# Rope products at other key tiles, and the shared-key maxima ending one tile sooner, in a four-layer transformer kernel

## The chip, the cores and the metric

The kernel runs on one core of one Trainium2 chip. The metric is device time in microseconds (us). A core has TensorE for matmuls (PE in the profile), VectorE (DVE), ScalarE (ACT), GpSimd (POOL) and SyncE (SP), which issues most DMAs. Each engine works through its own instructions in order; semaphores hold one engine back for another.

## The reference

Four layers, each `x + attention(layernorm(x)) + feed-forward(layernorm(x))`, on 1024 tokens of 256 features. The change touches only the two attentions of layer 0, both causal, with 16 heads of 16 features:

```python
# latent attention with rotary positions ("rope")
ql = x @ Wqd
q  = (ql @ Wqu)                      # 16 heads x 16
qr = apply_rope(ql @ Wqr, cos, sin)  # 16 heads x 64: x*cos + rotate_half(x)*sin
kr = apply_rope(x @ Wkr, cos, sin)   # one key of 64 for all heads
scores = (q @ k.T + qr @ kr.T) * scale
out = softmax(causal(scores)) @ v @ Wo
# feed-forward of layer 0: attention whose key and value are shared by all heads
k_shared, v_shared = the routed head's k and v, v weighted by the gate
att = softmax(causal(q @ k_shared.T / 4))
y = att @ v_shared                   # for each of 16 heads
```

## The kernel before, in words

The 16 heads of each attention go in groups of four. `GROUPS[0]` is the eight groups i = 0 to 7 of layer 0: even i are the latent attention (`is_mla`, here "rope groups"), odd i the shared-key attention (`is_shared`), in turn. Each group loops over eight key tiles kt of 128 keys. (i,kt) names a tile of this loop. For a tile PE computes transposed scores into psA (lines 1687 and 1688; a unit is one head for kt below 4 and two heads above), ACT turns them into exponentials in Pr (lines 912, 917), POOL masks the diagonal block (line 781), and PE multiplies with the values into psO (`values_product`, line 1725) one tile later. Since only queries from kt x 128 on are scored, later tiles are shorter.

The softmax needs each row's maximum beforehand. So, while group i runs, PE computes the plain scores of a group ahead once more into the two psD banks (`maxima_unit`, lines 1670 and 1672), in 38 units, and DVE reduces each unit (line 1204). `max_window` says beside which tiles the units of a group run, `beside` shares them out in proportion to the tiles' widths. A rope group's maxima run in tiles 0 to 4 of the shared-key group before it; a shared-key group's begin in tiles 5 to 7 two groups before it and end in the rope group before it. `max_end` is the tile at which they are complete. At that tile DVE negates the maxima (line 1209), PE transposes them (line 1678), DVE copies the row out (line 1222), and ACT sends it by DMA (`maxima_row`, lines 931 and 934) into the query operand, as one more row of it. For a shared-key group it is `Qs<-mrowb`. PE waits for it (`mrow_in`) before the group's first score.

Queries of the rope attention are rotated in products of two heads each, `rope` 0 to 7. 0 to 3 (heads 0 to 7) are made at the start. 4 to 7 (heads 8 to 15, for groups 4 and 6) are made beside the tiles of `ROPE_AT`: eight PE matmuls in four units (`rope_unit`, line 1604), four DVE products with cos and sin (line 1183), then on POOL, after that tile's mask, a sum (line 736), on ACT, after the next tile's exponentials, a rounded copy (line 944), and on POOL, after the next tile's mask, the remainder (line 741). SP stores both parts to HBM (`store_rotated`: `d_qr<-WB`, `d_qr<-xnT`), the remainder's product waiting in the places WB or xnT.

SP's program for a rope group i in 2 and 4: wait for and store products i+2 and i+3, wait until the stores have landed, wait until the scores of tile 3 of group i are filled, then load the first half of group i+2's high parts (`load_high`: `Qr<-d_qr`, `Qr<-d_qn`, `Kr<-d_kn`); once all scores of group i are filled, the second half and the rest. PE waits for the first half before the first maxima unit of group i+2, in tile 0 of group i+1. SP takes all this in order.

In group 6 POOL also carries the butterflies of a weight transform (line 792), two after each mask.

Of the kernel before, what the change touches and what calls it, by code (L numbers as in the profile page):

```python
# [53 lines left out]

def max_end(g):

    return 5


def is_mla(i):  # L60
# [4 lines left out]
def is_shared(i):  # L65

    return i < 2 * NG and i % 2 == 1
# [4 lines left out]
    return i // 2 if i < 2 * NG else i - 2 * NG  # L72


ROPE_AT = {(2, 0): 4, (2, 2): 5, (4, 0): 6, (4, 2): 7}
KV_AT = {(0, 0): range(0, NT // 2), (0, 1): range(NT // 2, NT)}
KEY_KT = 3

# [1 line left out]
def beside_products(i, kt):  # L80

    if (i, kt) in KV_AT:
        return [("kv", j) for j in KV_AT[i, kt]]
    if (i, kt) in ROPE_AT:
        return [("rope", ROPE_AT[i, kt], k) for k in range(4)]
    if (i, kt) == (2 * NG - 1, 1):
# [4 lines left out]
def max_window(i, first):  # L91

    if i == 1:
        return [(0, kt) for kt in range(KEY_KT, max_end(1))]
    tail = [(i - 2, kt) for kt in range(max_end(i - 1), NT) if i - 2 >= first and not is_mla(i)]
    return tail + [(i - 1, kt) for kt in range(max_end(i))]
# [24 lines left out]
def build(nc, ins, out):  # L121
    with ExitStack() as ctx:
# [575 lines left out]
        def _(pool):  # L698
# [34 lines left out]
            def rope_add(p):  # L733
                pool.wait_ge(d_drained, DU[f"rope{p}"])
                v, b = rope_place(p)
                pool.tensor_tensor(v, v, b, ALU.add).then_inc(rope_sum, 1)

            def rope_rest(p):
                pool.wait_ge(rope_high, p + 1)
                v, b = rope_place(p)  # L740
                pool.tensor_tensor(v.bitcast(F32R), v, b, ALU.subtract).then_inc(rope_low, 1)
# [34 lines left out]
            def mask_exponentials(i, kt):  # L776

                s = NT * i + kt
                pool.wait_ge(a_drained, scored(i, kt))
                block_ = Pr[:, (s % 2) * GH * T:(s % 2 + 1) * GH * T].rearrange("p (h t) -> p h t", h=GH)[:, :, tile_cols(kt)]  # L780
                pool.affine_select(out=block_, in_=block_, pattern=[[0, GH], [1, P]], compare_op=ALU.is_ge, fill=0.0,  # L781
                                   base=0, channel_multiplier=-1).then_inc(masked, 1)
# [15 lines left out]
            for i in GROUPS[0]:  # L798
                for kt in range(NT):
                    mask_exponentials(i, kt)  # L800
                    if (i, kt) in ROPE_AT:
                        rope_add(ROPE_AT[i, kt])
                    if (i, kt - 1) in ROPE_AT:
                        rope_rest(ROPE_AT[i, kt - 1])
                    if i == 1 and kt < 4:
# [1324 lines left out]
```

## Time and profile before

| | us |
|---|---|
| median of 3 runs | 992.88 |
| lowest, highest | 991.86, 996.1 |
| the profiled execution's own time | 994.7 |
| its span | 993.0 |
| PE busy | 862.0 (87%) |
| DVE busy | 555.9 (56%) |
| ACT busy | 386.8 (39%) |
| POOL busy | 224.9 (23%) |

The groups of layer 0 run from 93.7 us on; group 7 ends near 471 us. The mean granted TensorE clock is 0.914 of full speed.

How to read the views. The chain is the path of work that ended last, followed back from the end. A timeline row is the start, the length, engine and line, operation, out<-in with shapes, the count, and in brackets the engine's idle time before it with what ended it. A windows row is a stretch and its length, then the busy time (and instructions) of PE, PE's weight loads, DVE, ACT and POOL, then the granted clock of TensorE, the DMA engines' mean share and GB/s. A row by line and shape has the count, busy time, mean ns of one, and idle time before. A row of DMA queues has packets, MB and the share of the 16 engines. "q" behind an engine's name is its sequencer, which issues DMAs. Matmul lengths overlap, as they are pipelined; spacing of starts is the better measure.

### The profile page before, as it was taken

What the parts mean: (1) busy time and instruction counts of PE and PEld (TensorE: products, weight loads), DVE (VectorE), ACT (ScalarE), POOL (GpSimd) and SP (SyncE); (2) the same over time, 40 slices, a digit from 0 to 9 for tenths busy, and PEclk for the clock granted to TensorE, in tenths of its full rate; (3) what the DMA queues carried; (4) which work ended last, traced back from release to release, by engine and by line L of the source; (5) the groups of instructions that cost most, each with busy time, mean ns of one, the idle gap of its engine ahead of it and who ended that gap; (6) DMA issues with size and microseconds to landing.
All of it is one profiled execution on the core that took longest, in us unless ns stands there. A gap on an engine that the chain in (4) does not pass through costs nothing.

```text
span 993.0 us, 11940 instructions
## 1 busy us (share of the span) xinstructions
PE 862.0 (87%) x4799; PEld 505.4 (51%) x4799; DVE 555.9 (56%) x991; ACT 386.8 (39%) x476; POOL 224.9 (23%) x207
## 2 busy tenths in 40 slices
PE   4697979988999899987779998788999889888997
PEld 2354434444344434524448886533333258687776
DVE  4574486774677476512433453596777337934452
ACT  2504314534444454445351331205555754500340
POOL 2661002323013212523010100500111147600000
PEclk9878999999799889979789997968999989989899
DMA  6687216514721770020400002759000061000001
GB/s 174 130 174 225 34 33 107 112 49 105 129 34 43 145 179 2 2 71 1 149 0 1 1 1 88 147 108 130 2 2 1 2 222 43 0 1 1 1 1 43
DMA packets 35648, 66.82 MB, mean 67 GB/s; under 512 B 5908, under 2 KB 14652, under 8 KB 35524
## 3 DMA queue, kind: packets, MB, share of 16 engines
q1 hardware_dynamic: 35016, 65.92, 29.0%
q8 instruction: 38, 0.62, 0.3%
q10 hardware_dynamic: 576, 0.13, 0.1%
q14 instruction: 18, 0.15, 0.1%
HBM read 45.93 MB, written 16.29 MB: 63 GB/s over the span
## 4 chain that ended last, share of the span: by engine, by line
PE 63%; DVE 19%; DMA 6%; ACT 6%; POOL 2%; issue 2%; SPq 1%; ACTq 0%; DVEq 0%; POOLq 0%
PE psA L1604 11%; PE psD L1604 11%; PE psO L1725 10%; DVE mx L1204 9%; PE psD L1670 8%; PE psA L1688 7%; PE psO L1604 7%; PE psA L1687 3%; DMA Kr<-d_kn 3%; DVE hid_low L1518 2%; PE psD L1672 2%; PE psA L1636 1%; SPq L488 1%; ACT Pr L912 1%; PE psD L1736 1%
## 5 line engine op out<-in xcount | busy, mean ns | idle before, releaser
L1204 DVE TENSOR_REDUCE mx<-psD 128x1 f32<-128x512 f32 (+3 forms) x416 | 259.3, 659 | 122.9 <-PE psD L1672 88.3
L912 ACT ACTIVATE Pr<-psA 128x1024 f32<-128x1024 f32 (+3 forms) x192 | 161.9, 865 | 194.9 <-PE psA L1688 185.4
L781 POOL TENSOR_SCALAR_AFFINE_SELECT Pr<-Pr 128x512 f32<-128x512 f32 x96 | 61.0, 635 | 435.6 <-ACT Pr L912 349.6
L917 ACT ACTIVATE Pr<-psA 128x1024 f32<-128x1024 f32 (+3 forms) x96 | 63.5, 702 | 65.4 <-PE psA L1688 65.0
L1725 PE MATMUL psO<-Pr,Vh 128*32 128x512 f32 (+3 forms) x768 | 81.9, 507 | 3.7 <-POOL Pr L781 3.0
L1687 PE MATMUL psA<-Qr,Kr 128*128 128x512 f32 (+3 forms) x192 | 77.5, 417 | 3.7 <-DMA Qr<-mrow 3.7
L1672 PE MATMUL psD<-maskq,identb 128*128 128x128 bf16 x348 | 73.0, 234 | 0.0
L1688 PE MATMUL psA<-Qr,Kr 113*128 113x512 f32 (+3 forms) x192 | 66.5, 354 | 0.0
L1670 PE MATMUL psD<-Kg,Qs 96*128 96x512 bf16 (+3 forms) x192 | 56.2, 333 | 9.0 <-DVE mx L1204 6.9
L1670 PE MATMUL psD<-Kr,Qr 80*128 80x512 bf16 (+3 forms) x166 | 59.2, 390 | 5.2 <-DVE mx L1204 3.0
L1688 PE MATMUL psA<-Qs,Kg 97*128 97x512 bf16 (+3 forms) x192 | 51.3, 366 | 9.5 <-DMA Qs<-mrowb 4.3
L1670 PE MATMUL psD<-Ks,Qs 96*128 96x512 bf16 (+3 forms) x166 | 53.5, 351 | 4.6 <-DVE mx L1204 3.8
L1688 PE MATMUL psA<-Qs,Ks 97*128 97x512 bf16 (+3 forms) x192 | 45.8, 332 | 5.3 <-ACT Pr L912 3.3
L1670 PEld LDWEIGHTS psD<-Kg,Qs 96*128 96x128 bf16 x192 | 17.9, 97 | 57.8 <-DVE mx L1204 43.8
L1687 PEld LDWEIGHTS psA<-Qr,Kr 128*128 128x128 f32 x192 | 37.6, 196 | 18.2 <-ACT Pr L917 6.2
L1636 PE MATMUL psA<-identf,xn 128*128 128x128 f32 x96 | 21.6, 389 | 27.2 <-DVE xn L1169 26.7
L1670 PEld LDWEIGHTS psD<-Kr,Qr 80*128 80x128 bf16 x166 | 18.0, 109 | 50.2 <-DVE mx L1204 37.1
L1725 PE MATMUL psO<-Pr,Vg 128*32 128x512 f32 (+3 forms) x384 | 42.7, 525 | 0.6 <-POOL Pr L781 0.5
L1670 PEld LDWEIGHTS psD<-Ks,Qs 96*128 96x128 bf16 x166 | 16.4, 100 | 47.3 <-DVE mx L1204 42.2
L1672 PEld LDWEIGHTS psD<-maskq,identb 128*128 128x128 bf16 x348 | 36.8, 106 | 5.9 <-issue 3.3
L1688 PEld LDWEIGHTS psA<-Qr,Kr 113*128 113x128 f32 x192 | 37.3, 194 | 4.2 <-issue 1.9
L1604 PE MATMUL psA<-xnT,WA 128*128 128x512 f32 x56 | 32.2, 739 | 2.7 <-ACT xnT L877 2.2
(403 smaller groups left out, 1658.6 us busy)
## 6 DMA issues: line engine op xcount, KB each, us to landing
Qr<-d_qr SPq DMA_DIRECT2D x18, 512.0 KB, 12.3
d_qr<-WB SPq DMA_DIRECT2D x9, 512.0 KB, 2.6
Pr<-d_cb SPq DMA_DIRECT2D x8, 512.0 KB, 7.8
Qs<-d_gq SPq DMA_DIRECT2D x24, 128.0 KB, 4.8
Qs<-d_q SPq DMA_DIRECT2D x24, 128.0 KB
Ks<-d_k SPq DMA_DIRECT2D x24, 128.0 KB
Qr<-d_qn SPq DMA_DIRECT2D x18, 128.0 KB, 7.7
Kr<-d_kn SPq DMA_DIRECT2D x18, 128.0 KB, 8.5
```

Of the source, the lines that this page charges most:

```text
L781: pool.affine_select(out=block_, in_=block_, pattern=[[0, GH], [1, P]], compare_op=ALU.is_ge, fill=0.0, base=0, channel_multiplier=-1).the ...
L912: act.activation(place[:, h, q0:T], src[:, q0:T], ACT.Exp, scale=score_scale(i)).then_inc(a_drained, 1)
L917: act.activation(place[:, h:h + 2, q0:T], src[:, :, q0 - HALF:HALF], ACT.Exp, scale=score_scale(i)).then_inc(a_drained, 1)
L1204: dve.tensor_reduce(mx[:, j, part, h0:h0 + nh], src, AX, ALU.max).then_inc(d_drained, 1)
L1518: dve.tensor_tensor(hid2_low[:, m - DC, :], slot(Qs, m - DC), hid2_high[:, m - DC, :], ALU.subtract).then_inc(hid2_split, 1)
L1604: op = pe.matmul(dst, lhsT, rhs, start=start and k == 0, stop=stop and k == len(terms) - 1)
L1636: op = pe.transpose(dst[:, tile_cols(j)], src[:, j, c * P:(c + 1) * P], identf[:])
L1670: op = pe.matmul(dst[:, k * w:(k + 1) * w], q, kk, start=True, stop=not diagonal)
L1672: op = pe.matmul(dst[:, (k + 1) * w - P:(k + 1) * w], identb[:], maskq[:], start=False, stop=True)
L1687: pe.matmul(out_, second[0], second[1](lo, (half + 1) * HALF), start=True, stop=False)
L1688: op = pe.matmul(out_, k, q(lo, (half + 1) * HALF), start=second is None, stop=not (diagonal and mask))
L1725: op = pe.matmul(psO[h * VW:(h + 1) * VW, lo:hi], values(i, kt, h), e, start=kt == 0, stop=kt == last_kt, tile_position=(0, h * VW), skip_ ...
```

## The change

`max_end` is 4 instead of 5 for the shared-key groups 3, 5 and 7; for group 1 and all others it stays. So groups 2, 4 and 6 have no maxima units beside tile 4, the 38 units are shared out over one tile less, and the row is transposed and sent in tile 4. `ROPE_AT` puts rope products 4 and 6 beside tile 5 of groups 1 and 3, and 5 and 7 beside tile 0 of groups 2 and 4. Nothing is added or left out.

```diff
 def max_end(g):
 
-    return 5
+    return 4 if is_shared(g) and g > 1 else 5
...
-ROPE_AT = {(2, 0): 4, (2, 2): 5, (4, 0): 6, (4, 2): 7}
+ROPE_AT = {(1, 5): 4, (2, 0): 5, (3, 5): 6, (4, 0): 7}
```

Units of maxima beside each tile of group 2 (the same in 4 and 6), and of tile 7 of the group before:

| | (1,7) | (2,0) | (2,1) | (2,2) | (2,3) | (2,4) |
|---|---|---|---|---|---|---|
| before | 1 | 8 | 8 | 6 | 5 | 5 |
| now | 2 | 9 | 8 | 8 | 6 | 0 |

PE in group 2 where the maxima of group 3 are transposed (`identf,mneg`), before. The 128x384 rows are scores of tile 5, the 128x256 row of tile 6:

```order
L1687 MATMUL psA<-Qr_51,Kr_52 128x384
L1688 MATMUL psA<-Qr,Kr 128x384
L1678 MATMUL psD<-identf,mneg 32x128
L1725 MATMUL psO<-Pr,Vh 32x512 x4
L1687 MATMUL psA<-Qr_51,Kr_52 128x256
L1688 MATMUL psA<-Qr,Kr 128x256
```

And now. The 128x512 rows are scores of tile 4:

```order
L1687 MATMUL psA<-Qr_51,Kr_52 128x512
L1688 MATMUL psA<-Qr,Kr 128x512
L1678 MATMUL psD<-identf,mneg 32x128
L1725 MATMUL psO<-Pr,Vh 32x128 x4
L1725 MATMUL psO<-Pr,Vh 32x512 x4
L1687 MATMUL psA<-Qr_51,Kr_52 128x384
L1688 MATMUL psA<-Qr,Kr 128x384
```

The transposition stands ahead of tile 5's scores, not behind them.

DVE from the last maxima of group 2, in (1,4), to the outputs of group 1 in (2,1), before. L1183 are the rope products, `mneg` and `mrow` group 2's row:

```order
L1209 TENSOR_REDUCE mneg<-mx 128x32
L1222 CAST mrow<-psD 32x128
L1204 TENSOR_REDUCE mx<-psD 128x4
L1204 TENSOR_REDUCE mx<-psD 128x2 x2
L1204 TENSOR_REDUCE mx<-psD 128x1 x3
L1183 TENSOR_TENSOR WB<-psD,gate 128x512 x4
L1204 TENSOR_REDUCE mx<-psD 128x1 x9
```

And now:

```order
L1209 TENSOR_REDUCE mneg<-mx 128x32
L1222 CAST mrow<-psD 32x128
L1183 TENSOR_TENSOR WB<-psD,gate 128x512 x4
L1204 TENSOR_REDUCE mx<-psD 128x4
L1204 TENSOR_REDUCE mx<-psD 128x2 x2
L1204 TENSOR_REDUCE mx<-psD 128x1 x4
L1183 TENSOR_TENSOR WB<-psD,gate 128x512 x2
L1183 TENSOR_TENSOR xnT<-psD,gate 128x512 x2
L1204 TENSOR_REDUCE mx<-psD 128x1 x8
```

Product 4 stands right behind group 2's row, in (1,5), and product 5 (the one with `xnT`) in (2,0), where 4 stood.

ACT from group 2's row to its tile 3, before. L944 is a rope product's rounded copy; L917 with 2x256 and 2x128 are the exponentials of (1,6) and (1,7), L912 with 1024, 896, 768, 640 those of (2,0) to (2,3):

```order
L931 DMA Qr<-mrow 1x32x128
L917 ACTIVATE Pr<-psA 128x2x256 x2
L917 ACTIVATE Pr<-psA 128x2x128 x2
L912 ACTIVATE Pr<-psA 128x1024 x4
L962 ACTIVATE OT<-psO 128x1024
L912 ACTIVATE Pr<-psA 128x896 x4
L944 ACTIVATE WB<-WB 128x1024
L912 ACTIVATE Pr<-psA 128x768 x4
L912 ACTIVATE Pr<-psA 128x640 x4
L944 ACTIVATE xnT<-WB 128x1024
```

And now:

```order
L931 DMA Qr<-mrow 1x32x128
L917 ACTIVATE Pr<-psA 128x2x256 x2
L944 ACTIVATE WB<-WB 128x1024
L917 ACTIVATE Pr<-psA 128x2x128 x2
L912 ACTIVATE Pr<-psA 128x1024 x4
L962 ACTIVATE OT<-psO 128x1024
L912 ACTIVATE Pr<-psA 128x896 x4
L944 ACTIVATE xnT<-WB 128x1024
L912 ACTIVATE Pr<-psA 128x768 x4
L912 ACTIVATE Pr<-psA 128x640 x4
```

The first copy now stands between the exponentials of (1,6) and (1,7), the second behind (2,1). On POOL the sum stands ahead of the mask of (1,6) and the remainder ahead of that of (1,7). SP's instructions and their order are the same.

## Rows read from the trace of the kernel before

**Rows 1.** chain that ended last, shares of the span by engine
```profile
PE 63%; DVE 19%; DMA 6%; ACT 6%; POOL 2%; issue 2%; SPq 1%; ACTq 0%; DVEq 0%; POOLq 0%
```

**Rows 2.** windows: group 0 to 1, group 2 to 3 (two rows), group 4 to 5
```profile
156.92:173.51 16.59, 15.22 (x110) 6.42 (x109) 12.69 (x22) 9.12 (x11) 3.85 (x5) 1.00 0.94 157
241.97:267.55 25.58, 21.86 (x110) 8.94 (x109) 13.02 (x22) 9.38 (x12) 1.91 (x3) 0.67 1.00 169
245.87:267.55 21.68, 20.34 (x96) 8.46 (x97) 13.02 (x22) 8.62 (x10) 1.27 (x2) 0.61 0.98 170
334.47:359.79 25.32, 21.79 (x110) 8.88 (x109) 13.01 (x22) 9.38 (x12) 1.90 (x3) 0.66 1.08 174
```

**Rows 3.** timeline of PE, end of group 2
```profile
231.74 0.59 PE L1687 MATMUL psA<-Qr,Kr 128*128 128x512 f32 x1
...
235.94 0.39 PE L1670 MATMUL psD<-Kg,Qs 96*128 96x512 bf16 x1
...
236.22 0.38 PE L1670 MATMUL psD<-Kg,Qs 96*128 96x512 bf16 x1
...
238.06 0.28 PE L1678 MATMUL psD<-identf,mneg 128*32 128x128 f32 x1
...
242.25 0.64 PE L1725 MATMUL psO<-Pr,Vh 128*32 128x256 f32 x8
245.17 0.61 PE L1688 MATMUL psA<-Qs,Kg 97*128 97x512 bf16 x2 [2.28 <-DMA Qs<-mrowb]
246.50 0.29 PE L1670 MATMUL psD<-Kr,Qr 80*128 80x128 bf16 x1 [0.73 <-DMA Kr<-d_kn]
```

**Rows 4.** timeline of SP's queue, group 2
```profile
213.62 2.82 SPq L488 DMA_DIRECT2D d_qr<-WB  x2
...
236.03 0.32 SPq L488 DMA_DIRECT2D d_qr<-WB  x1
238.64 0.58 SPq L488 DMA_DIRECT2D Qr<-d_qr  x1
```

**Rows 5.** chain in order of time, group 2: start, length
```profile
233.63 2.38 POOL WB L741
```

**Rows 6.** DMA queues from 242.0 to 243.3; timeline of ACT
```profile
q1 hardware_dynamic: 164, 0.28, 109.9%
...
238.79 0.51 ACTq L934 DMA_DIRECT2D Qs<-mrowb  x1
```

**Rows 7.** windows: (0,4)-(0,5), (1,5)-(1,7), (2,2), (4,0), (4,2), (4,4), (6,0), (6,2)
```profile
139.25:155.07 15.82, 13.01 (x72) 6.11 (x70) 10.72 (x19) 3.67 (x5) 1.27 (x2) 0.89 0.19 34
188.24:196.12 7.88, 6.97 (x63) 3.72 (x62) 4.78 (x10) 3.25 (x6) 1.91 (x3) 1.00 0.36 113
214.91:227.15 12.24, 10.42 (x51) 4.85 (x50) 8.74 (x14) 3.24 (x5) 1.94 (x3) 0.86 0.17 70
290.15:300.05 9.90, 9.06 (x49) 5.77 (x48) 7.91 (x13) 4.90 (x6) 0.73 (x2) 1.00 0.44 53
308.93:319.64 10.71, 8.90 (x51) 4.49 (x50) 8.71 (x14) 3.25 (x5) 1.94 (x3) 1.00 0.20 80
325.93:330.00 4.07, 4.07 (x34) 2.28 (x33) 2.94 (x5) 1.93 (x4) 2.96 (x2) 1.00 0.49 198
382.38:389.78 7.40, 6.89 (x41) 4.31 (x40) 5.44 (x9) 4.89 (x5) 0.73 (x2) 1.00 0.01 2
398.65:405.45 6.80, 6.50 (x42) 3.03 (x40) 5.13 (x10) 3.25 (x4) 0.14 (x2) 1.00 0.01 2
```

**Rows 8.** DVE by line and shape, 190 to 240 us
```profile
L1204 DVE TENSOR_REDUCE mx<-psD 128x1 f32<-128x512 f32 x24 | 15.7, 688 | 5.8 <-PE psD L1670 4.1 <-PE psD L1672 1.7
...
L1183 DVE TENSOR_TENSOR WB<-psD,gate 128x512 f32<-128x512 f32 x6 | 3.9, 686 | 1.5 <-PE psD L1604 1.5
```

**Rows 9.** timelines of POOL and PE, end of group 6
```profile
417.64 0.64 POOL L781 TENSOR_SCALAR_AFFINE_SELECT Pr<-Pr 128x512 f32<-128x512 f32 x1 [0.50 <-ACT Pr L917]
...
427.05 1.03 PE L1688 MATMUL psA<-Qs,Kg 97*128 97x512 bf16 x2 [3.79 <-POOL Pr L781]
```

## The prediction

> **What bounds the kernel now.** I read the page's chain first. PE carries 63% of it; the next shares are DVE 19% and DMA 6% [rows 1]. So PE sets the end, and time goes where PE stands still or runs at the low clock. I then laid windows over the tiles of the first attention, above all where one head group hands over to the next. (i,kt) below is key tile kt of group i; groups 0, 2, 4, 6 are rope groups, 1, 3, 5, 7 shared-key groups.
>
> The windows over the handovers are the finding. Tile 7 of group 0 and the first two tiles of group 1 take 16.59 us together, at clock 1.00. The same work takes 25.58 us from group 2 to 3 and 25.32 us from group 4 to 5, at a mean clock of 0.67. Of the 25.58, tile 7 is 3.90 (25.58 less 21.68) and the two tiles after it 21.68, at clock 0.61. PE's busy time grows as well, from 15.22 to 21.86 us [rows 2], so this is slow matmuls, not only waiting. Of its two levels, 1.2 and 2.4 GHz, the clock sits at the lower for most of that stretch.
>
> What stands ahead of it is in PE's timeline. After the last product of group 2 (242.25) PE idles 2.28 us for the row of maxima, `Qs<-mrowb`, and after two matmuls another 0.73 us for `Kr<-d_kn` [rows 3]. Both are DMAs. From group 0 to 1 PE is idle 1.37 us of 16.59 in all, and the clock stays up [rows 2].
>
> Where do the two come from? SP's queue gives the second. The high parts of group 4's queries and keys (`Qr<-d_qr`, `Qr<-d_qn`, `Kr<-d_kn`) are issued from 238.64 on, behind the store `d_qr<-WB` of rope product 5 at 236.03 [rows 4]. The chain shows what the store waited for: POOL's subtraction, 2.38 us from 233.63 [rows 5]. The load is in when PE goes on at 246.50 [rows 3]. The first wait: ACT issues `Qs<-mrowb` at 238.79, and PE goes on at 245.17, 6.4 us later. It is one row. The load went out 0.15 us before it and has the DMA engines full: 164 packets of SP's queue in the 1.3 us from 242.0 [rows 3, 4, 6]. So the late load makes both waits.
>
> **The change part by part.** P is the time at which PE starts the scores of (2,4); before it is 231.74, and PE wants group 3's row when the product at 242.25 is done, 2.28 us before 245.17: at 242.9, P+11.1 [rows 3].
>
> Rope products move. Each is 8 PE matmuls, 4 DVE products of 0.69 us, two POOL passes of 2.4 us, an ACT copy, and two stores on SP [rows 5, 8]. In (4,2) the tile takes 10.71 us; (6,2), with the same scores and maxima and no rope product, takes 6.80. In group 2 it is 12.24 us at clock 0.86 [rows 7]. So it costs 3.9 and 5.4 us there. Not all of that goes: DVE is busy 8.71 against 5.13 us, 3.6 more, of which the four products are 2.8; the other 0.8 is DVE's output of the group before, stretched beside POOL's remainder pass of the product of tile 0, and that product stays. So 3.1 and 4.6 are saved. What it costs at its new place, (1,5) and (3,5), no row shows. Below is what PE alone does more in (4,0), which has a product, than in (6,0), which has none: 9.06 - 6.89 = 2.2 us busy [rows 7]. Above are the four DVE products, 2.8 us. I take 2.5, the whole difference of these two tiles, 9.90 - 7.40. Tile (2,0) keeps one product (5 in place of 4), so it is even. Sum: (2.5 - 3.1) + (2.5 - 4.6) = **-2.7 us**, bounds -4.9 (2.2, and all of 3.9 and 5.4) to -2.1 (2.8).
>
> What is queued behind the moved work: on POOL the masks of (1,6) and (1,7) now stand behind the two passes, and on ACT the exponentials of (1,7) stand behind the copy. Tiles (1,5) to (1,7) take 7.88 us together [rows 7]. (1,5) starts at 188.24, and by my estimate its scores and transposition take 1.7 us. Then DVE has the product done at 192.7 (4 x 0.69), POOL's sum ends at 195.1, ACT's copy (some 1 us) behind the exponentials of (1,6) at 196.4, POOL's difference at 198.8 and the mask of (1,7), 0.64 us [rows 9], at 199.4. PE wants that mask after two score units (1 us each) and the four rope pairs (2.2 us) of (2,0), which starts near 197: at 201. So it is hidden with about 1.6 us to spare; without that cover each us late is a us of PE, twice.
>
> Five maxima units per rope group move. The 38 units of a group are shared out by the tiles' widths, and tile 4 drops out: one more in (1,7), one in (2,0), two in (2,2), one in (2,3), none in (2,4). A unit, one psD bank, is 0.28 us on PE (235.94 to 236.22) and 0.69 us on DVE [rows 3, 8]. Where PE is the pacing engine it costs 0.28, where DVE is, 0.69. DVE is busy 5.4 of 7.4 us in (6,0) and 5.1 of 6.8 in (6,2) [rows 7], so neither holds alone; I take 0.45. Added 5 x 0.45 = 2.25; saved in (2,4), which is all PE (4.07 busy of 4.07), 5 x 0.28 = 1.4. Net +0.85 each for groups 2 and 4. Group 6 is different: POOL's butterflies fill it from (6,4) on, PE waits 3.79 us for POOL before 427.05, and only the 0.50 us that POOL idles before 417.64 can be squeezed [rows 9]. There it is 2.25 - 0.5 = +1.75. Sum **+3.4 us**, bounds +0.9 and +7.0 (at 0.28 and 0.69 a unit).
>
> Group 3's and 5's row is sent a tile sooner. In (2,4) PE does eight score matmuls of 0.24 us, then the transposition, at P+2.1; DVE should have the last maximum (0.69 us) and the negation by P+1.3. From transposition to issue took 0.73 us (238.06 to 238.79) [rows 3, 6], so the row goes out at P+2.8. Rope product 5 now stands where 4 stood, and 4 was stored at 213.62 to 216.44 [rows 4], P-15; so SP's load goes as soon as (2,3)'s scores are filled, P+0.2, and is in by P+8.1 (238.64 to 246.50 was 7.9 us). PE needs it at about P+10.3. The row collides with that load again, so I give it the whole 6.4 us it took now: P+9.2. PE wants it at P+11.1 less the 1.4 us of moved units, P+9.7. That leaves 0.5 us. Both waits go. What is late next is the second half of the load, sent when group 2's scores end; group 0's handover runs so already, within its 16.59 us.
>
> With the wait gone I expect the clock to stay up as at the end of group 0. So each of the two handovers falls to 16.59 us: from 25.58, -9.0; from 25.32, -8.7. Sum **-17.7 us**, of which the waits of 2.28 and 0.73 us, twice, are 6.0 and the rest, 11.7, is clock. If the clock does not come back, the 6.0 is all that is left. Group 0's handover is the only such row at full clock, so this term rests on it.
>
> Total: -2.7 + 3.4 - 17.7 = **-17.0 us**. The profiled execution is 994.7 us with a span of 993.0, so its successor would be 977.7; the median shown, 992.88, is 1.8 below it, and 992.9 - 17.0 = **975.9 us**.
>
> **Rivals.**
> A. *The stall shrinks but stays, and the clock with it.* The load moves forward together with the row, and it has 2.6 us more of head start; my margin is 0.5 us. If the row comes 0.7 us after P+9.7 at both handovers, the waits drop from 2.3 to 0.7, the clock still falls: -2.7 + 3.4 - 2 x (1.6 + 0.7) = -3.9, 989.0 us. For it: the 6.4 us that one row takes beside the load. Against: most of the load is through by then. The Trainium skill ("DMA: Bandwidth & Descriptors", Queues, rings and completion order) says that an engine's semaphore increment lands only after every earlier write of that engine, across its queues. By that rule more of the load now stands ahead of the row, yet the row is bound by the load's own end, P+8.1, and not by 6.4 us: the spare would be 1.6 us in place of 0.5, and A would deserve 0.05 in place of the chance below. The trace agrees in that the row came 1.3 us before the load's end, not after; I keep the chance that the 6.4 us gives.
> B. *One handover is mended, the other not*, or a short clock fall appears in a rope group: -17.0 + 7 to 9, about 984 us.
> C. *Slower: the crowded tiles pace PE by DVE and the clock falls inside the rope groups.* Tiles 0 to 3 of groups 2, 4 and 6 hold 31 units instead of 27; each makes PE idle 0.41 us (0.69 - 0.28) where DVE paces. It decides from where PE's pauses there add up to what the handover had. Price: 6.6 us of clock (PE busy 21.86 - 15.22 at the handover) in each of three groups and 15 x 0.24 = 3.6 us over my 0.45: -17.0 + 19.8 + 3.6 = +6.4, 999.3 us. For it: (0,4) and (0,5), after 38 units in two tiles, are at 0.89, (2,2) at 0.86 [rows 7]. Against: these falls cost 1 to 2 us, not 6.6, and groups 4 and 6 keep 1.00 with PE busy 83 to 96% of a tile.
> D. *Nothing changes at the handover* because SP does not send the load sooner: it still stands behind group 1's end and the store; then +0.7 is left, 993.6 us. The store of 216.44 is some 15 us before P, which speaks against it.
>
> **Numbers.** Forecast 0.67, its own range 970 to 981 (the terms' bounds give 971.2 to 980.1, and a run varies by 1 or 2); A 0.14, B 0.10, C 0.05, D 0.04. About 0.5%, 5 us, is what a measurement of this kernel tells from no change. Forecast, B and a third of A are faster: 0.82. D and the rest of A are the same: 0.13. Slower: 0.05. To leave no more than 2 in 10 out, 968 to 988.
>
> **What would show it.** In the profile after: no wait for `Qs<-mrowb` or `Kr<-d_kn` at the end of groups 2 and 4, clock 1.00 there, the three tiles near 16.6 us; the load of group 4 issued some 7 us sooner against the last tile and well apart from the stores of `d_qr`; (2,2) near 7.8 us, (1,5) to (1,7) near 10.5, (2,4) near 2.9; the wait for POOL at the start of group 7 longer than 3.8 us. I am wrong if the clock is still half after those handovers, or if DVE is busy over 90% in tiles 0 to 3 of the rope groups.

## The result, and the profile after

The changed kernel takes 977.8 us (median of 4 runs, 975.59 to 980.72) against 993.2 us (991.86 to 996.1) for the kernel before beside it. The ratio is 0.984, 95% interval 0.981 to 0.988: 15.4 us faster, where 17.0 were forecast. A second set of runs of the changed kernel gave 977.0 (ratio 0.983, 0.980 to 0.986). In the profiled executions the span falls from 993.0 to 974.5 us; these two executions took 994.7 and 976.2 us, 1.5 us above and 1.6 us below the medians.

PE still carries the chain, and the share of DMA in it is a point smaller than in [rows 1]. Shares of the span by engine, of after:

```profile
PE 64%; DVE 21%; ACT 5%; DMA 5%; POOL 2%; issue 2%; SPq 1%; DVEq 0%; ACTq 0%; POOLq 0%
```

The two handovers come first, since the forecast stood on them. Windows over tile 7 of groups 2 and 4 and the two tiles behind it, of after (stretch and length, then busy time of PE, PE's weight loads, DVE, ACT, POOL, the granted clock, DMA share, GB/s):

```profile
241.41:258.00 16.59, 15.29 (x110) 6.41 (x109) 12.70 (x22) 9.12 (x12) 1.90 (x3) 1.00 0.93 160
326.56:343.22 16.66, 15.18 (x110) 6.41 (x109) 12.70 (x22) 9.12 (x11) 1.90 (x3) 1.00 0.96 153
```

Both were 25 us and more at clocks 0.67 and 0.66 [rows 2]. They now take what group 0's handover took, with the DMA engines nearly as full as before (0.93 and 0.96 against 1.00 and 1.08).

PE's timeline at the end of group 2, of after, shows the waits gone:

```profile
232.72 0.47 PE L1687 MATMUL psA<-Qr,Kr 128*128 128x512 f32 x1
...
234.68 0.27 PE L1678 MATMUL psD<-identf,mneg 128*32 128x128 f32 x1
...
241.69 0.64 PE L1725 MATMUL psO<-Pr,Vh 128*32 128x256 f32 x8
242.26 0.60 PE L1688 MATMUL psA<-Qs,Kg 97*128 97x512 bf16 x2
242.70 0.22 PE L1670 MATMUL psD<-Kr,Qr 80*128 80x128 bf16 x1
```

P, the start of (2,4)'s scores, is 232.72. From the last product (241.69) PE goes straight on to group 3's scores (242.26) and group 4's first maxima (242.70), with no bracket behind either, where [rows 3] has 2.28 and 0.73 us. SP's queue and ACT's, of after:

```profile
219.87 0.32 SPq L488 DMA_DIRECT2D d_qr<-WB  x1
232.70 0.58 SPq L488 DMA_DIRECT2D Qr<-d_qr  x1
```

```profile
235.40 0.51 ACTq L934 DMA_DIRECT2D Qs<-mrowb  x1
```

The last part of product 5 goes to its store 12.8 us before the load, so the load goes at P (forecast P+0.2) and the row at P+2.7 (forecast P+2.8). The load's first DMA is 2.7 us ahead of the row's; before it was 0.15 us ahead [rows 4, 6].

The tiles that the units and products moved into and out of, of after: (1,5) to (1,7), (2,2), (2,4), (4,2). A tile's window, here and in [rows 7], runs from the start of ACT's first exponential of the tile to that of the next one, so an ACT instruction that is put in at the border moves the border:

```profile
187.55:198.60 11.05, 9.73 (x73) 4.93 (x72) 7.94 (x15) 4.09 (x7) 5.40 (x4) 1.00 0.24 78
...
218.57:227.42 8.85, 7.11 (x46) 3.31 (x44) 7.05 (x12) 3.24 (x5) 1.59 (x2) 1.00 0.25 101
234.00:237.17 3.17, 3.17 (x27) 1.90 (x26) 0.28 (x1) 1.94 (x2) 0.70 (x2) 1.00 0.92 217
303.73:312.56 8.83, 7.09 (x46) 3.33 (x44) 7.05 (x12) 3.24 (x4) 1.59 (x2) 1.00 0.26 103
```

Against [rows 7], (1,5) to (1,7) grew from 7.88 to 11.05 us, (2,2) and (4,2) fell from 12.24 and 10.71 to 8.85 and 8.83, and (4,4) (like (2,4)) from 4.07 to 3.17.

Where the 18.5 us between the two spans lie, by windows from one group's start to another's:

| stretch | before | after | difference |
|---|---|---|---|
| groups 1 and 2 | 87.39 | 85.17 | -2.2 |
| groups 3 and 4 | 92.27 | 85.15 | -7.1 |
| group 5 | 44.24 | 37.72 | -6.5 |
| group 6 | 40.54 | 41.99 | +1.4 |
| group 7, tiles 0 to 6 | 40.38 | 39.09 | -1.3 |
| all else | 688.2 | 685.4 | -2.8 |

The change touches the first four rows, together -14.4 us. The last two do the same work in both kernels. Of the -4.1 there, -1.3 is the clock in group 7's second tile (0.86 of full speed and 10.12 us, where it was 0.76 and 11.41). The second set of runs has a profiled execution of its own, and in it this tile is at 0.77 and 11.33 us, and the first four rows are together -13.7. So no meaning is read into the last two rows.

### The profile page after: what moved, and what is told of

Same layout as the page of the kernel before. It is cut to its first block, busy times and chain, and to the rows that moved or that the text cites. A ratio compares the mean times of both kernels' runs of the same rounds, so it can differ in the third digit from the quotient of the medians.

```text
span 974.5 us, 11941 instructions
## 1 busy us (share of the span) xinstructions
PE 845.6 (87%) x4799; PEld 498.0 (51%) x4799; DVE 555.5 (57%) x991; ACT 386.6 (40%) x476; POOL 224.4 (23%) x207
## 4 chain that ended last, share of the span: by engine, by line
PE 64%; DVE 21%; ACT 5%; DMA 5%; POOL 2%; issue 2%; SPq 1%; DVEq 0%; ACTq 0%; POOLq 0%
PE psD L1604 11%; PE psA L1604 11%; DVE mx L1204 10%; PE psO L1725 10%; PE psD L1670 8%; PE psA L1688 7%; PE psO L1604 7%; PE psA L1687 4%; DMA Kr<-d_kn 2%; DVE hid_low L1518 2%; PE psA L1636 2%; PE psD L1672 1%; SPq L488 1%; PE psD L1736 1%; ACT Pr L912 1%
## 5 line engine op out<-in xcount | busy, mean ns | idle before, releaser
L912 ACT ACTIVATE Pr<-psA 128x1024 f32<-128x1024 f32 (+3 forms) x192 | 161.7, 865 | 176.0 <-PE psA L1688 166.3
L917 ACT ACTIVATE Pr<-psA 128x1024 f32<-128x1024 f32 (+3 forms) x96 | 63.4, 702 | 68.6 <-PE psA L1688 68.3
L1672 PE MATMUL psD<-maskq,identb 128*128 128x128 bf16 x348 | 69.4, 225 | 0.0
L1670 PE MATMUL psD<-Kr,Qr 80*128 80x512 bf16 (+3 forms) x166 | 53.1, 346 | 5.0 <-DVE mx L1204 3.6
L1688 PE MATMUL psA<-Qs,Kg 97*128 97x512 bf16 (+3 forms) x192 | 46.0, 335 | 5.2 <-POOL Pr L781 3.8
L1725 PE MATMUL psO<-Pr,Vg 128*32 128x512 f32 (+3 forms) x384 | 40.5, 502 | 0.1
```

What stands on the lines that cost most here:

```text
L912: act.activation(place[:, h, q0:T], src[:, q0:T], ACT.Exp, scale=score_scale(i)).then_inc(a_drained, 1)
L917: act.activation(place[:, h:h + 2, q0:T], src[:, :, q0 - HALF:HALF], ACT.Exp, scale=score_scale(i)).then_inc(a_drained, 1)
L1670: op = pe.matmul(dst[:, k * w:(k + 1) * w], q, kk, start=True, stop=not diagonal)
L1672: op = pe.matmul(dst[:, (k + 1) * w - P:(k + 1) * w], identb[:], maskq[:], start=False, stop=True)
L1688: op = pe.matmul(out_, k, q(lo, (half + 1) * HALF), start=second is None, stop=not (diagonal and mask))
L1725: op = pe.matmul(psO[h * VW:(h + 1) * VW, lo:hi], values(i, kt, h), e, start=kt == 0, stop=kt == last_kt, tile_position=(0, h * VW), skip_ ...
```

## Experiments

My theory was that the late load alone makes both waits: the product stored late holds the load back, and the load holds the row back. The rival was that the row needs its earlier start, which only the moved maxima give. The first two kernels do one half of the change each. Each ratio is to runs of the kernel before that were made beside that kernel: their median is 994.5 us for the first four kernels, 993.1 for the next four and 993.5 for the last, on three different chips. Medians from different chips are therefore compared through their ratios, and small differences by the tiles of the traces.

**The products moved alone.**

```diff
-ROPE_AT = {(2, 0): 4, (2, 2): 5, (4, 0): 6, (4, 2): 7}
+ROPE_AT = {(1, 5): 4, (2, 0): 5, (3, 5): 6, (4, 0): 7}
```

> Only the four rope products are moved; every shared-key group's maxima end at tile 5 as before. My theory (T1): the pause at the end of groups 2 and 4 is made by the late load, which both comes late itself and holds up the row of maxima; the pause brings the low clock. With the rope products moved the load goes at P+0.2 and is through when the row is issued at P+7, so the row takes 2 to 3.5 us instead of 6.4 and PE, which wants it at P+11.1, does not wait. Handovers 16.6 us each at clock 1.00, and the cost of the moved maxima units (in the changed kernel some 1.9 us in groups 2 and 4, 1.5 in group 6) is not paid: 972.5 us, 970 to 976, which is less than the changed kernel's 977.8. Rival (T2): the row is late because it is sent late; a row takes 6.4 us here whatever runs beside it. Then it is seen at P+13.4, PE waits 2.3 us, the clock falls as before, 988 to 992 us.

Measured: 975.17 us (972.15 to 977.08), ratio 0.980 (0.977 to 0.984). Window of this kernel over the handover from group 2 to 3:

```profile
240.48:257.29 16.81, 15.17 (x110) 6.34 (x109) 12.70 (x22) 9.12 (x11) 1.91 (x3) 1.00 0.94 156
```

The handover is mended with the maxima left where they were. ACT's queue has the row at 237.30:

```profile
237.30 0.51 ACTq L934 DMA_DIRECT2D Qs<-mrowb  x1
```

and the DMA queues of this kernel, from 238.4 to 238.7, hold its 48 packets and nothing else (packets, MB, share of the 16 engines):

```profile
q10 hardware_dynamic: 48, 0.01, 13.8%
```

P is 230.24 in this trace, so the row goes out at P+7.1, as in the kernel before, and PE takes it 4.0 us later (241.33) without a wait; before, PE stood ready 4.1 us after the issue and waited. The row's packets are through 1.4 us after its issue when no load stands beside it; before, with the load beside it, they ran in the same 1.3 us as 164 packets of the load [rows 6], 3.2 to 4.4 us after the issue, and PE went on another 1.9 us later. The rival falls: the row needs no earlier start. The medians of the two kernels, 975 and 977 to 978, are too close to tell what the other half of the change costs, since the intervals of the ratios overlap; the traces do tell it (below).

**The maxima moved alone.**

```diff
 # from the changed kernel
-ROPE_AT = {(1, 5): 4, (2, 0): 5, (3, 5): 6, (4, 0): 7}
+ROPE_AT = {(2, 0): 4, (2, 2): 5, (4, 0): 6, (4, 2): 7}
```

> Only max_end is 4 for groups 3, 5 and 7; the rope products stay beside (2,0), (2,2), (4,0), (4,2). T1: the row, issued at P+2.8 with nothing beside it, comes in time, but the load still goes at about P+6.9 and is in at P+14.8, while PE wants it at P+10.3; the pause is then some 4.5 us, all of it for Kr<-d_kn, at the low clock as before. The moved units cost 5 us and what tile 4 saves is waited away: 996 to 1002 us. T2 (the sooner row is what mends the handover): the clock stays up, 978 to 983 us.

Measured: 997.71 us (993.78 to 1001.91), ratio 1.004 (1.001 to 1.006). SP's queue and PE's timeline, end of group 2, of this kernel:

```profile
236.91 0.32 SPq L488 DMA_DIRECT2D d_qr<-WB  x1
239.53 0.58 SPq L488 DMA_DIRECT2D Qr<-d_qr  x1
```

```profile
242.37 0.60 PE L1688 MATMUL psA<-Qs,Kg 97*128 97x512 bf16 x2
247.68 0.29 PE L1670 MATMUL psD<-Kr,Qr 80*128 80x128 bf16 x1 [4.71 <-DMA Kr<-d_kn]
```

The row now comes in time (no wait at 242.37), yet the wait for the load is 4.71 us (4.10 at the second handover). The stall has only changed its name, since the load still stands behind the store. The handover takes 26.41 us at clock 0.68.

**The load sent later, everything else as in the changed kernel.** Two kernels move only the point from which SP sends the first half of the load.

```diff
-sp.wait_ge(a_filled, scored(i, NT // 2 - 1))
+sp.wait_ge(a_filled, scored(i, 5 if i > 0 else NT // 2 - 1))
```

> The changed kernel, but SP sends the first half of group 4's and 6's high parts only when the scores of tile 5 of groups 2 and 4 are filled, not those of tile 3. It makes the pause again by itself, without touching PE, DVE, ACT or POOL. T1 (a pause brings the low clock): the load is in near P+13.5, PE wants it at P+10.3, so it waits some 3 us twice, and the two tiles after it run at a mean clock near 0.6 and cost 6.6 us more each: 2 x (3 + 6.6) = +19, 995 to 999 us. Rival (T3: the clock fell for something else that the change took away, as the rope matmuls of (2,2) or the denser tile 4): only the wait returns, 982 to 985 us, clock 1.00 at the handovers.

Measured: 995.14 us (991.85 to 999.23), ratio 1.000 (0.998 to 1.003): the whole gain is gone. SP's queue and PE's timeline of this kernel:

```profile
237.70 0.58 SPq L488 DMA_DIRECT2D Qr<-d_qr  x1
```

```profile
245.65 0.29 PE L1670 MATMUL psD<-Kr,Qr 80*128 80x128 bf16 x1 [2.94 <-DMA Kr<-d_kn]
```

There is one such wait per handover, 2.94 and 2.86 us. The handover's window shows what comes with it:

```profile
241.25:266.65 25.40, 21.74 (x110) 8.88 (x109) 13.02 (x22) 9.38 (x12) 1.91 (x3) 0.66 0.99 169
```

8.8 us more than in the changed kernel, of which 2.9 are the wait; the other 5.9 come with the lower clock. So the rival to a pause as the cause (T3, 982 to 985 us with the clock at 1.00) falls. With 4 in place of 5:

> As load_at_5, but with the scores of tile 4. The load goes at about P+3.1, 0.3 us behind the row, so it collides with the row as in the kernel before. T1: the row comes 6.4 us after its issue, P+9.2, just in time, the load at P+11, so PE waits under 1 us. Whether so short a pause brings the low clock is open: if not, 978 to 981 us; if so, 990 to 993 us.

Measured: 979.62 us (974.59 to 982.82), ratio 0.984 (0.980 to 0.988). SP's queue and PE's timeline of this kernel:

```profile
235.02 0.58 SPq L488 DMA_DIRECT2D Qr<-d_qr  x1
```

```profile
242.86 0.23 PE L1670 MATMUL psD<-Kr,Qr 80*128 80x128 bf16 x1
...
335.91 0.63 PE L1670 MATMUL psD<-Kr,Qr 80*128 80x512 bf16 x2 [0.53 <-DMA Kr<-d_kn]
```

The first tile after the handover is just served, and the clock stays at 1.00 over both handovers. One wait of 0.53 us for `Kr<-d_kn` shows inside group 5. It is not the price of the later load: the changed kernel waits at the same place, 0.24 us in its first trace and 0.74 us in its second. From the load's issue to PE going on took 8.15 us with the maxima alone, 7.95 with the load sent at 5, and 7.86 in the kernel before [rows 3, 4]; with 4 it took 7.84 at most. So in the changed kernel, where nobody waits for it, the load is in near 232.70 + 8 = 240.7 by this estimate, 2.0 us before PE wants it (242.70). Moving the load by 2.3 us (4) costs nothing that shows, by 5.0 us (5) everything.

These kernels also show by themselves what the load does to the row, since only the load's place differs between them. ACT's queue and the DMA queues, with 5 and then with 4 (from 236.3 to 236.7, and from 238.4 to 239.95):

```profile
235.24 0.51 ACTq L934 DMA_DIRECT2D Qs<-mrowb  x1
q10 hardware_dynamic: 48, 0.01, 10.2%
```

```profile
235.50 0.52 ACTq L934 DMA_DIRECT2D Qs<-mrowb  x1
q1 hardware_dynamic: 168, 0.28, 108.6%
q10 hardware_dynamic: 48, 0.01, 5.4%
```

With the load 2.5 us behind the row, the row's last packet ends 1.4 us after the row's issue. With the load 0.5 us ahead of it, it ends 4.4 us after, and with the load 2.7 us ahead, in the changed kernel, 4.0 us after.

**Which tile the product goes to.** Both kernels have the maxima as in the kernel before, and differ from the first experiment by one line.

```diff
-ROPE_AT = {(1, 5): 4, (2, 0): 5, (3, 5): 6, (4, 0): 7}
+ROPE_AT = {(1, 6): 4, (2, 0): 5, (3, 6): 6, (4, 0): 7}
```

> rope_only, but products 4 and 6 beside tile 6 of groups 1 and 3, not tile 5. In tile 5 the product made the three tiles (1,5) to (1,7) 3.16 us longer (7.88 to 11.04), where I had 2.5. Theory H1: that is because its four units all stand in one run behind the transposition, so that PE and DVE alternate over two banks with nothing between. In tile 6 they are spread, two at each of the first two points, with the scores and the values product between: tiles 5 to 7 take 10.2 to 10.6 us and the total is 1 us lower than rope_only. Rival H2: a product costs DVE its four times 0.69 us and PE its 2 wherever it stands in these short tiles: 11.0 us or, as the copy and the second POOL pass come nearer to the masks of (1,7) and (2,0), more, up to 12; total equal to rope_only or 1 to 2 us above.

Measured: 971.42 us (970.44 to 972.88), ratio 0.978 (0.975 to 0.981). Tiles (1,5) to (1,7) of this kernel:

```profile
186.82:197.71 10.89, 10.00 (x73) 5.34 (x72) 7.66 (x15) 4.32 (x7) 4.23 (x4) 1.00 0.30 87
```

They take 10.89 us against 11.04 in the first experiment; (2,0) behind them takes 9.25 against 9.90, and (4,0) the same. Together that is 0.8 us a group, 1.6 in all. The split between the two windows misleads, though. ACT's copy now stands ahead of the exponentials of (2,0) and moves the border to 197.71, while PE starts that tile at 195.79. PE and ACT, of this kernel:

```profile
187.79 0.28 PE L1678 MATMUL psD<-identf,mneg 128*32 128x128 f32 x1 [0.74 <-DVE mneg L1209]
...
195.79 0.48 PE L1687 MATMUL psA<-Qr,Kr 128*128 128x512 f32 x1
...
196.75 1.06 ACT L944 ACTIVATE WB<-WB 128x1024 fp32r<-128x1024 f32 x1 [1.02 <-POOL WB L736]
```

From the transposition in (1,5) to the first score of (2,0) PE takes 8.00 us here, 8.79 in the first experiment and 5.64 in the kernel before, and (2,0) itself takes 9.4 us in all three by PE's starts. So the product costs 2.4 us spread out and 3.15 us as one block, and the three tiles did become 10.2 us (7.88 + 2.36), as H1 has it. The product also stands in another tile here, which this run does not separate from the spreading. The median is 3.7 us lower, but the two kernels ran on different chips and the intervals of their ratios overlap, so no more than the 1.6 us is shown.

```diff
-ROPE_AT = {(1, 5): 4, (2, 0): 5, (3, 5): 6, (4, 0): 7}
+ROPE_AT = {(2, 0): 4, (2, 1): 5, (4, 0): 6, (4, 1): 7}
```

> rope_only, but products 4 and 5 beside (2,0) and (2,1), 6 and 7 beside (4,0) and (4,1): nothing in groups 1 and 3, and product 5 still stored before tile 3's scores are filled. My theory: what matters is only that the store is through by then. The handovers stay at 16.6 us and clock 1.00. The product costs about 2.5 us in (2,1), as in (2,0), so the groups are 0.6 us shorter each: about 974 us. Rival: POOL now has two passes of 2.4 us behind the mask of (2,1), beside DVE's output products, of which one already takes 2.0 in place of 0.42 us beside such a pass; each further one stretched costs up to 1.6 us, and the mask of (2,2) comes late: 976 to 980 us, with the load still in time.

Measured: 975.08 us (974.67 to 978.45), ratio 0.982 (0.979 to 0.986), not to be told from the first experiment's 0.980. The handovers stay mended, since the store is early enough from (2,1) as well. But (2,1) and (2,2) take 10.93 and 11.02 us, and the clock dips in the second of them. Window of (2,2):

```profile
215.62:226.64 11.02, 8.65 (x44) 3.58 (x42) 7.18 (x10) 4.08 (x5) 3.94 (x3) 0.85 0.20 78
```

Groups 1 and 3 save 6.5 us together against the first experiment, and groups 2 and 4 pay 9.0 us for two products in neighbouring tiles. By the tiles this place is 2.5 us worse, as the rival had it, though the total came out below the rival's 976.

**The wait for POOL at the start of group 7.** From the first experiment's kernel, the butterflies begin at (5,5), not at (6,0).

```diff
-                    if i == 6:
-                        if kt == 0:
+                    at = NT * i + kt - (NT * 5 + 5)
+                    if at >= 0:
+                        if at == 0:
...
-                        for step in steps_1[2 * kt:2 * kt + 2]:
+                        for step in steps_1[2 * at:2 * at + 2]:
```

> rope_only, and POOL's 14 butterfly steps start at tile (5,5) instead of (6,0). A third pause is left in all kernels so far: PE waits some 3.8 us for POOL's mask of (6,7), and tiles (7,0) and (7,1) run at a clock of 0.56 and 0.87. My theory that a pause brings the low clock says: with POOL done by (6,3) the wait goes, (7,0) takes 4.8 to 5.5 us in place of 8.5 (ACT is busy 4.8 of it), (7,1) 9 to 10, and (6,6) to (6,7) 0.9 less; total 969 to 972 us. Rival: POOL's passes now stand before masks in tiles 5 to 7 of group 5 (3.8 us of work and 2.3 of passes) and before that of (6,3), and hold PE up there, and the clock falls at (5,7) or (6,3) in place of (7,0): 974 to 980 us.

Measured: 969.25 us (966.64 to 971.72), ratio 0.976 (0.973 to 0.979). PE's wait of 3.7 us for POOL is gone, and (7,0) takes 4.53 us, not 8.50. Group 6 is 0.3 us shorter, and (7,1) is unchanged, 10.12 us at clock 0.86. That is 4.2 us over groups 5 to 7.

**Both together**: the products at (1,6) and (3,6), the butterflies from (5,5).

> Moves the products of (1,5) and (3,5) to (1,6) and (3,6), and POOL's butterflies of the weight transform to start at (5,5) in place of (6,0); the shared-key groups' maxima still end at tile 5. Each edit alone, beside rope_only (975.17): the products -3.7 us (971.42), the butterflies -5.9 us (969.25). The traces account for 1.6 us of the first (0.8 us less in each of (1,5) to (2,0) and (3,5) to (4,0)) and for about 6 of the second (no wait for POOL at the start of group 7, and its clock stays up). My theory: the two touch different tiles (groups 1 to 4 against 5 to 7), so they add as the traces say: 967.6, range 965 to 970. Rival 1: they add as the medians say, 965.5. Rival 2: part of what the products' move gave in the median was the clock in group 7, which the butterflies give as well: 969, no better than the butterflies alone. In the trace: no wait for POOL over 0.6 us, (7,0) near 4.5 us, (1,5) to (1,7) 10.9, (2,0) 9.25.

Measured: 967.35 us (963.58 to 969.1), ratio 0.972 (0.969 to 0.975), the fastest of all. Tile (7,1) of this kernel:

```profile
405.96:414.44 8.48, 7.96 (x40) 2.88 (x38) 4.37 (x12) 3.61 (x5) 0.64 (x1) 1.00 0.20 77
```

It came out near the 967.6 that I expected, but partly by luck. I had counted 6 us for the butterflies, and their trace shows 4.2: 975.2 - 1.6 - 4.2 is 969.4. The trace of the combination has another 1.6 us in (7,1), at clock 1.00 where it was 0.86. The interval of the ratio, 963 to 969 us, also reaches both rivals' figures (965.5 and 969), so the medians decide nothing; the tiles do: (2,0) takes 9.25 us and (1,5) to (1,7) 10.90, as expected, so the gain of the moved products is there beside that of the butterflies. A difference of 2 us between two medians of four to six runs should not be added up.

**The changed kernel once more**, run together with the last three single edits.

> The changed kernel once more, on the same chip as the others: 976 to 980 us, some 3.7 us above rope_only by the tiles of the two traces (1.1 us in each of groups 2 and 4, 1.5 us in group 6). If the moved maxima units cost nothing, it would equal rope_only's 975.

Measured: 977.0 us (974.45 to 979.08), ratio 0.983 (0.980 to 0.986), the same as the first time.

## Why the prediction was right, and where not

| term | forecast | by the traces |
|---|---|---|
| rope products moved | -2.7 (-4.9 to -2.1) | -0.4 |
| five maxima units moved, three groups | +3.4 | +3.6 |
| two handovers | -17.7 | -17.65 |
| sum | -17.0 | -14.4 |

**Handovers: right, mechanism and size.** 25.58 to 16.59 and 25.32 to 16.66. Group 0's handover was the right pattern. The steps came as forecast: the load's issue at P, transposition at P+2.0, row at P+2.7, PE at the row's turn at P+9.5 (forecast P+9.7). The price of the row was somewhat too high. These are the DMA queues of after from 237.3 to 239.5:

```profile
q1 hardware_dynamic: 57, 0.08, 36.0%
q10 hardware_dynamic: 48, 0.01, 6.9%
```

The row's 48 packets end at P+6.7, 4.0 us after its issue. The 6.4 us of the prediction run to PE going on, and where PE did wait for such a row in the kernel before, it went on 1.9 and 1.8 us after the last packet at the two handovers (0.9 us at the row of group 0, 84.40). With 1.9 us the row is there at P+8.6, 0.9 us ahead of PE's turn, where the prediction had 0.5: rival A did not happen, but its margin was nearly as narrow as stated. The rule of the Trainium skill that I set against it ("DMA: Bandwidth & Descriptors", Queues, rings and completion order) gave the row the load's own end as its bound, with 1.6 us to spare. The trace agrees to that extent: the row's last packet is ahead of the load's estimated end of P+8.0. The rest of that rule, the order of the increments, no run here shows. The second half of the load, named as next to be late, is next: the waits of 0.24 and 0.74 us for `Kr<-d_kn` in (5,1) of the changed kernel's two traces come some 10 us after the first half was in by the same estimate (issue at 317.84 and 316.52, and 8 us more).

Of the tile lengths named as signs, (2,4) came near (3.17 us for 2.9), (1,5) to (1,7) did not (11.05 for 10.5) and (2,2) neither (8.85 for 7.8); the last two belong to the terms below.

Rival B did not happen: both handovers are mended, in both traces.

Rival D (nothing changes, since the load stands behind the store) is what happened with the maxima alone (997.7 us, where D had 993.6), and it was the store's place that decided it. Rival C (the crowded tiles bring the clock down) did not happen with 31 units in four tiles: tiles 0 to 7 of groups 2, 4 and 6 are at 1.00 in both traces of the changed kernel. On a small scale it did happen with two products next to each other, and once in (4,2) of the kernel with the load at 5 (last section), for 1.6 us and not the 6.6 that I priced.

**Maxima: right.** Against the first experiment, where only they differ, groups 2 and 4 are 1.07 and 1.10 us longer (0.85 forecast) and group 6 1.43 (1.75); the second trace gives 1.09, 1.10 and 1.54. They buy nothing in this kernel: they are worth their price only if the row is the late one, and the moved store alone had made it early enough. PE's start of group 7, of after, answers to [rows 9]:

```profile
411.97 1.03 PE L1688 MATMUL psA<-Qs,Kg 97*128 97x512 bf16 x2 [3.81 <-POOL Pr L781]
```

The single wait stayed at 3.8, and the time that POOL holds PE back grew elsewhere: (6,7) takes 3.03 us for 2.45.

**Rope products: mis-sized.** This is the step that failed: "Above are the four DVE products, 2.8 us. I take 2.5." It costs 3.16 us, outside the bounds. Tile lengths in the kernel before and with the products alone moved:

| | before | products alone |
|---|---|---|
| (1,5) to (1,7) | 7.88 | 11.04 |
| (2,0) | 9.91 | 9.90 |
| (2,2) | 12.24 | 7.94 |
| (2,4) | 4.07 | 4.37 |
| (4,2) | 10.71 | 7.91 |

PE's timeline in (1,5), of after:

```profile
188.52 0.28 PE L1678 MATMUL psD<-identf,mneg 128*32 128x128 f32 x1 [0.74 <-DVE mneg L1209]
188.56 0.48 PE L1604 MATMUL psD<-lat_parts,wq_high 128*128 128x512 f32 x1
...
191.45 1.07 PE L1725 MATMUL psO<-Pr,Vg 128*32 128x512 f32 x8
...
193.87 0.28 PE L1670 MATMUL psD<-Kg,Qs 96*128 96x256 bf16 x1 [0.45 <-DVE mx L1204]
```

DVE's, of after:

```profile
189.38 1.34 DVE L1183 TENSOR_TENSOR WB<-psD,gate 128x512 f32<-128x512 f32 x2 [0.16 <-PE psD L1604]
190.91 1.34 DVE L1183 TENSOR_TENSOR WB<-psD,gate 128x512 f32<-128x512 f32 x2 [0.18 <-PE psD L1604]
193.12 2.52 DVE L1204 TENSOR_REDUCE mx<-psD 128x4 f32<-128x512 f32 x4 [0.87 <-PE psD L1672]
```

The product stands as one block, four pairs of matmuls without a score or a maximum between them. PE passes through it in 2.89 us (188.56 to 191.45), starting a pair every 0.65 to 0.85 us, where pairs that wait for nothing follow each other in 0.45 (196.81 to 197.26 in the kernel with the product at (1,6)); DVE works from 189.38 to 192.25 and then idles 0.87 us behind the values product; then PE waits 0.45 us for DVE again. The two engines take turns with what they could do beside each other. My upper bound counted DVE's busy time as if nothing around the block could lie idle. A better upper bound for an added block is its time on the engine that paces it and the idle time at its ends: here 2.87 us on DVE and 0.87 us idle, 3.7. The run with the product at (1,6) bears this out: spread between scores and a values product it costs 2.4 us, within the bounds of the prediction.

The rest of this term: (2,2) and (4,2) saved 4.30 and 2.80 where 4.6 and 3.1 were forecast. (2,4) and (4,4) got 0.30 longer and (2,3) and (4,3) 0.12 shorter, for which I had nothing. For PE tile 4 is the same, 4.73 us from its first score to that of tile 5 in both kernels: ACT's copy of product 5 no longer stands ahead of its exponentials, so its window begins sooner. In all the term is 2.3 us off, nearly the whole of the 2.6 between the sums. The masks behind the moved product came as forecast. POOL's mask of (1,7), of after,

```profile
199.15 0.64 POOL L781 TENSOR_SCALAR_AFFINE_SELECT Pr<-Pr 128x512 f32<-128x512 f32 x1
```

starts at 199.15 (forecast 199.4), and PE waits for none of the masks there.

The forecast of 975.9 against 977.8 is closer than the sum deserves, and that is luck: the medians differ by 1.0 us more than the -14.4 of the traces explains, and the spans by 4.1. Of these 4.1, 3.1 are the distance of the two profiled executions from their medians.

## What to carry to other kernels

When an engine waits for two transfers in a row, look for one late issue behind both, and ask what stands ahead of it in its queue: here moving one store by a few tiles was the whole gain, and the second half of the change cost 3.6 us by the traces for a row that was already early enough. Price a stall of the matmul engine with the clock that follows it, by a like place that runs without the stall. Bound an added block by the engine that paces it plus the idle time at its ends, not by its busy time, and spread it if the order allows. Before a gain is put down to a tile, see by which engine's starts the tile is cut.

## What the runs showed of the hardware that was not expected

**How little it takes to lose the clock, and how much it takes back.** One wait of 2.94 us costs another 5.9 us of slow matmuls (the 25.40 us window above). One of 4.71 us costs no more: 26.41 us in all, 5.1 beside the wait. Waits of 0.53 and 0.74 us cost nothing beside themselves. Between them lies one of 1.52 us, which the changed kernel has in (2,2) and (4,2), with both tiles at clock 1.00 in both of its traces. The kernel with the load at 5 has the same work and the same waits there; its (2,2) is at 1.00, too, but its (4,2) is not. PE's wait in (2,2), of after, and the window of (4,2) of the kernel with the load at 5:

```profile
220.93 0.39 PE L1670 MATMUL psD<-Kg,Qs 96*128 96x512 bf16 x1 [1.52 <-DVE otmp L1234]
```

```profile
312.37:322.79 10.42, 8.68 (x46) 3.85 (x44) 7.05 (x12) 3.25 (x4) 1.58 (x2) 0.84 0.22 88
```

That is 1.6 us more than the 8.83 of the changed kernel. So the same stretch of work can keep the clock or lose some of it from one execution to the next, and where it turns stays open.

**Two engines on one memory.** DVE's timeline and POOL's in (2,2), of after, the output of group 1 (L1234 reads PSUM and SBUF, L1239 two operands in SBUF):

```profile
217.55 0.42 DVE L1234 TENSOR_TENSOR otmp<-psD,rec 128x256 f32<-128x256 f32 x1
218.00 2.12 DVE L1239 TENSOR_TENSOR x<-x,otmp 128x256 f32<-128x256 f32 x1
...
220.91 0.43 DVE L1239 TENSOR_TENSOR x<-x,otmp 128x256 f32<-128x256 f32 x1
```

```profile
217.46 2.38 POOL L741 TENSOR_TENSOR WB<-WB,xnT 128x1024 fp32r<-128x1024 f32 x1 [0.32 <-ACT xnT L944]
```

The same instruction takes 0.43 us alone and 2.12 beside POOL's pass, and ends 0.28 us after that pass does (219.84). The product with one operand in PSUM is not held up by it. The Trainium skill ("SBUF — State Buffer", SBUF: two separate sides) has the rule: a VectorE operation with two inputs in SBUF and a GpSimd operation take their shared port pair in turn, each for the whole instruction. The trace agrees, with 0.42 us of work held for 1.7. This is the stretch that the forecast counted at 0.8 us in (2,2) and in (4,2), as staying there; with the products moved alone (2,2) takes 7.94 us and (4,2) 7.91 against 6.80 in (6,2) [rows 7], so it was 1.1. The 0.3 us between is what the two tiles saved less than forecast.
